# The last rows of a fused two-layer kernel: another order of quantising steps, and a deviation that moves from the rows into the scales

## What is computed

```python
x = x + _L1_attn_ref(_layernorm(x), ...)          # 16 heads of 128, causal, per half of 256 x 2 rows
# last layer, on n = layernorm(x):
x_max   = max(abs(n), axis=row)
x_scale = maximum(x_max / 127, 1e-12)
x_q     = clip(round(n / x_scale), -128, 127)     # int8
y       = (x_q @ w_q.T) * x_scale * w_scale + bias
x       = x + y
```

## Time and profile before

| | |
|---|---|
| median of 3 runs | 505.29 us (504.79 to 505.61) |
| the profiled execution's own time | 505.88 us |
| its span in the profile | 504.1 us, 8912 instructions |
| mean granted TensorE clock | 0.991 of full speed |
| busy PE, PEld | 482.8 us (96%), 429.8 us (85%) |
| busy DVE, ACT, POOL | 378.2 us (75%), 295.4 us (59%), 282.5 us (56%) |

### The profile page before, as it was taken

One profiled execution on the slowest core, in us unless ns is written; L12 is line 12 of the kernel. 1 busy time (PEld: TensorE's weight loads), 2 busy tenths in 40 slices (PEclk: granted clock), 3 DMA queues, 4 the chain that ended last, 5 costly groups with the idle time before them and its releaser, 6 DMA issues.

```text
span 504.1 us, 8912 instructions
## 1 busy us (share of the span) xinstructions
PE 482.8 (96%) x3020; PEld 429.8 (85%) x3020; DVE 378.2 (75%) x964; ACT 295.4 (59%) x694; POOL 282.5 (56%) x378
## 2 busy tenths in 40 slices
PE   8999999999999977899999999999999999999984
PEld 7888998899888856799888999899889989899972
DVE  2776776775746578788779888788878897667897
ACT  2355336535554645676667676667757766655663
POOL 1344244323665556786667786777767796511344
PEclk9999999999999999999999999999999999999996
DMA  9900000000010017564864764764765654100002
GB/s 278 380 22 2 1 0 1 0 1 1 24 42 1 0 46 184 159 187 109 213 182 127 195 181 114 210 179 122 202 178 149 177 170 131 36 1 1 0 2 83
DMA packets 54380, 51.58 MB, mean 102 GB/s; under 512 B 3520, under 2 KB 49728, under 8 KB 54336
## 3 DMA queue, kind: packets, MB, share of 16 engines
q1 hardware_dynamic: 53248, 49.98, 34.7%
q10 hardware_dynamic: 1088, 1.05, 0.6%
HBM read 32.92 MB, written 18.09 MB: 101 GB/s over the span
## 4 chain that ended last, share of the span: by engine, by line
PE 71%; DVE 13%; POOL 4%; issue 4%; DMA 3%; ACT 3%; SPq 1%; DVEq 0%; POOLq 0%; ACTq 0%
PE bank L405 19%; PE bank L407 18%; PE bank L406 18%; PE bank L700 3%; PE bank L698 3%; PE bank L699 3%; POOL HID_lo L1156 2%; DMA Wv_sb<-wv 2%; DVE BT L1535 2%; PE bank L628 1%; PE bank L627 1%; DVE SM L1516 1%; PE bank L709 1%; ACT E L906 1%; DMA turned_dram<-BT 1%
## 5 line engine op out<-in xcount | busy, mean ns | idle before, releaser
L1187 POOL TENSOR_TENSOR PT_lo<-MV,PT_hi 128x512 fp32r<-128x512 f32 (+1 forms) x104 | 91.5, 909 | 51.5 <-ACT PT_hi L998 51.1
L987 ACT ACTIVATE PR<-SM,nmax 128x128 f32<-128x128 f32 (+3 forms) x128 | 72.0, 563 | 62.6 <-DVE nmax L1516 62.1
L1132 POOL TENSOR_TENSOR E_lo<-E,E_hi 128x512 fp32r<-128x512 f32 x24 | 31.0, 1297 | 54.0 <-ACT E_hi L911 46.8
L1516 DVE CUSTOM_DVE_ANT_0 SM<-bank,causal 128x384 f32<-128x384 f32 (+3 forms) x102 | 54.0, 530 | 9.3 <-PE bank L700 6.4
L405 PE MATMUL bank<-XT_hi,W_hi 128*128 128x512 f32 x128 | 52.3, 409 | 5.2 <-DVE V_lo L1498 3.7
L998 ACT CAST PT_hi<-MV 128x512 fp32r<-128x512 f32 (+1 forms) x104 | 42.1, 453 | 19.6 <-DMA MV<-turned_dram 19.2
L1535 DVE STREAM_TRANSPOSE BT<-PR 128x128 f32<-128x128 f32 (+1 forms) x104 | 48.2, 492 | 5.6 <-POOL PR L1171 3.8
L407 PE MATMUL bank<-XT_hi,W_lo 128*128 128x512 f32 x128 | 50.5, 394 | 0.0
L406 PE MATMUL bank<-XT_lo,W_hi 128*128 128x512 f32 x128 | 50.2, 392 | 0.0
L406 PE MATMUL bank<-PT_lo,V_hi 128*128 128x128 f32 (+3 forms) x130 | 41.5, 319 | 0.0
L407 PE MATMUL bank<-PT_hi,V_lo 128*128 128x128 f32 (+3 forms) x130 | 41.5, 319 | 0.0
(11 more groups left out here) (189 smaller groups left out, 1602.6 us busy)
## 6 DMA issues: line engine op xcount, KB each, us to landing
MV<-turned_dram SPq DMA_DIRECT2D x104, 160.0 KB, 3.2
turned_dram<-BT SPq DMA_DIRECT2D x26, 384.0 KB, 2.9
stage<-pack SPq DMA_DIRECT2D x32, 256.0 KB, 3.9
turned_dram<-BT SPq DMA_DIRECT2D x26, 256.0 KB, 3.3
X<-x SPq DMA_DIRECT2D x2, 512.0 KB, 8.9
wraw<-wupT SPq DMA_DIRECT2D x1, 1024.0 KB, 9.6
wraw<-wgateT SPq DMA_DIRECT2D x1, 1024.0 KB, 11.5
wraw<-wdownT SPq DMA_DIRECT2D x1, 1024.0 KB, 13.7
```

The lines of the kernel that those rows point to most:

```text
L987: act.activation(PR[:, c, 0:(c + 1) * P], SM[:, c % 2, 0:(c + 1) * P], ACT.Exp, bias=nmax1[:, c:c + 1], scale=-1.0, accum_out=sum1[:, c:c ...
L1132: pool.tensor_tensor(E0_lo[:, m, :], E0[:, m, :], E0_hi[:, m, :], ALU.subtract).then_inc(e0_lo, 1)
L1187: pool.tensor_tensor(by_quad(PT_lo[w % 2], c), moved_part(w, c), by_quad(PT_hi[w % 2], c), ALU.subtract).then_inc(mv_lo, 1)
L1516: dve.tensor_tensor_reduce(SM[:, c % 2, 0:n], s_bank(w, c)[:, 0:n], mask, 1.0, HIGHEST, ALU.add, ALU.min, nmax1[:, c:c + 1]).then_inc(s_ma ...
```

## The change

Four things are changed.

1. On DVE, N2 and N3 move from the end of window 29 to behind S2 of that window, and X0, X1, X2 move from window 31 (behind T0 T1) to the end of window 29. `clip_first`, now called `clip_rounded(0)`, moves from behind the last window into window 31 as X3, behind T0 T1. On ACT, R0 moves to behind T0 T1 of window 31, and X0 ahead of A1. On PE, I0 moves ahead of P1 and F1, with a wait for `o_free`.
2. Half 1 is no longer normalised by DVE. DVE writes the negative means of two tiles (`row_means`), and ACT writes x - mean (`centre`, steps N0 and N1, either side of I1). `centred_absmax` takes the maximum, and `centred_scale` puts rs into both the scale and the inverse scale: four small instructions for each pair of tiles in place of two.
3. GpSimd rounds tiles 4 and 5: two `tensor_scalar` instructions, times the inverse scale plus the rounding constant. DVE then clips them with `clip_rounded(1)`. `clip_above` and `clip_below` are no longer called.
4. GpSimd adds the bias to tiles 4 to 7 of X only when ACT has read them.

```diff
-            WINDOWS - 1: steps("T0 T1 B0 T2 A0 T3 P0 F0 A1 P1 F1 I0 I1")}
+            WINDOWS - 1: steps("T0 T1 B0 T2 A0 T3 P0 F0 A1 I0 P1 F1 I1")}
...
-            WINDOWS - 1: steps("T0 T1 B0 T2 A0 T3 R0 A1 X0 I0 I1")}
+            WINDOWS - 1: steps("T0 T1 R0 B0 T2 A0 T3 X0 A1 I0 N0 I1 N1")}
...
-            WINDOWS - 3: steps("T0 T1 S0 W2 N0 Q0 T2 T3 S1 N1 S2 R0 K1 N2 S3 A0 R1 N3"),
+            WINDOWS - 3: steps("T0 T1 S0 W2 N0 Q0 T2 T3 S1 N1 S2 N2 N3 R0 K1 S3 A0 R1 X0 X1 X2"),
...
-            WINDOWS - 1: steps("T0 T1 X0 X1 X2 B0 T2 A0 T3 O0")}
+            WINDOWS - 1: steps("T0 T1 X3 B0 T2 A0 T3 O0")}
...
             def int8_turn(t0, t1):
 
+                if t0 == 0:
+                    pe.wait_ge(o_free, WINDOWS - 1)
...
+            def centre(g):
+
+                for t in range(*GROUPS[g]):
+                    act.wait_ge(ln_mean, g)
+                    act.activation(XN[:, t % CT, :], X[:, t, :], ACT.Identity, bias=ln_nm[:, t % CT:t % CT + 1],
+                                   scale=1.0).then_inc(centred, 1)
...
-                pool.wait_ge(ln_norm, CT * k + c1)
+                if k < 7:
+                    pool.wait_ge(ln_norm, CT * k + c1)
...
             rstd(7, 2, CT)
+            pool.wait_ge(q_inv, 2)
+            pool.wait_ge(q_round, 1)
+            for t in range(*GROUPS[1]):
+                last = pool.tensor_scalar(XQ1[:, t % CT, :], XN[:, t % CT, :], xinv[:, t:t + 1], ROUND, ALU.mult, ALU.add)
+            last.then_inc(q_clip, 1)
+            pool.wait_ge(centred, 2)
             add_bias(7, qb_bc, 0, 2)
             pool.wait_ge(q_round, 4)
+            pool.wait_ge(centred, CT)
             add_bias(7, qb_bc, 2, CT)
...
+            def row_means(g):
+                c0, c1 = (t - CT for t in GROUPS[g])
+                dve.tensor_scalar(ln_nm[:, c0:c1], ln_mv[:, c0:c1, 0], -1.0, None, ALU.mult).then_inc(ln_mean, 1)
+
+            def centred_absmax(g):
+                t0, t1 = GROUPS[g]
+                dve.wait_ge(centred, t1 - CT)
+                dve.tensor_reduce(xam[:, t0:t1], XN[:, t0 - CT:t1 - CT, :], AX.X, ALU.max,
+                                  apply_absolute_value=True).then_inc(q_absmax, 1)
+
+            def centred_scale(g):
+
+                t0, t1 = GROUPS[g]
+                rows, rs = slice(t0, t1), ln_rs[:, t0 - CT:t1 - CT]
+                done = 3 * g - 2
+                dve.wait_ge(q_absmax, g + 1)
+                dve.wait_ge(ln_rstd, 7 + g)
+                dve.scalar_tensor_tensor(xs[:, rows], xam[:, rows], 1.0 / QMAX, rs, ALU.mult, ALU.mult).then_inc(q_scale, 1)
+                dve.wait_ge(q_scale, done + 1)
+                dve.tensor_scalar(xs[:, rows], xs[:, rows], 1e-12, None, ALU.max).then_inc(q_scale, 1)
+                dve.wait_ge(q_scale, done + 2)
+                dve.reciprocal(xinv[:, rows], xs[:, rows]).then_inc(q_scale, 1)
+                dve.wait_ge(q_scale, done + 3)
+                dve.tensor_tensor(xinv[:, rows], xinv[:, rows], rs, ALU.mult).then_inc(q_inv, 1)
...
-            def clip_first():
-                dve.wait_ge(q_clip, 1)
-                dve.tensor_scalar(XQ2[:], XQ1[:], ROUND + QMAX, ROUND + QMIN, ALU.min, ALU.max).then_inc(q_round, 1)
+            def clip_rounded(g):
+                t0, t1 = GROUPS[g]
+                c = slice(t0 % CT, t0 % CT + t1 - t0)
+                dve.wait_ge(q_clip, g + 1)
+                if g == 1:
+                    dve.wait_ge(q_ready, CT)
+                dve.tensor_scalar(XQ2[:, c, :], XQ1[:, c, :], ROUND + QMAX, ROUND + QMIN, ALU.min,
+                                  ALU.max).then_inc(q_round, 1)
...
-            b0_quantise = (token_absmax, token_scale, token_inverse)
+            b0_quantise = (token_absmax, token_scale, token_inverse, clip_rounded)
...
             ln_variance(7, 0, 2)
+            row_means(1)
             z_low_half(1)
-            clip_first()
...
             ln_variance(7, 2, CT)
-            ln_normalise(7, 0, 2)
-            token_absmax(1)
-            token_scale(1)
-            token_inverse(1)
-            ln_normalise(7, 2, CT, 1)
-            clip_above(1)
-            token_absmax(2)
-            clip_below(1)
-            token_scale(2)
-            token_inverse(2)
+            row_means(2)
+            centred_absmax(1)
+            centred_scale(1)
+            centred_absmax(2)
+            centred_scale(2)
+            clip_rounded(1)
```

More of the change, by code:

```diff
@@ L96, in build @@
         ln_rs = sb("ln_rs", [P, CT])
+        ln_nm = sb("ln_nm", [P, CT])
         w_abs = sb("w_abs", [P, 3])
@@ L212, in build @@
         ln_rstd, ln_norm = sem("ln_rstd"), sem("ln_norm")
+        ln_mean, centred = sem("ln_mean"), sem("centred")
         xt_psum, xt_hi, xt_lo = sem("xt_psum"), sem("xt_hi"), sem("xt_lo")
@@ L1078, in window @@
                         round_first()
+                    elif kind == "N":
+                        centre(c + 1)
                     elif kind == "X":
```

## The result

The changed kernel took 508.31 us in the median of 7 runs (507.31 to 509.84), against 505.29 (504.79 to 507.00) for the kernel before in as many runs beside it: a ratio of 1.0058, 95% interval 1.0042 to 1.0073. It is slower; the forecast was 505.6 with a range up to 506.6. Its profiled execution took 507.31 us, with a span of 505.5.

A forecast was written before the change was run, and what follows sets the result against it. It took PE and DVE as full at the attention's end, with DVE's order setting the end. Terms 0.54 + 0.20 + 0.12 - 0.56 = +0.30 us, carried over to the median of 505.29, gave 505.6, range 504.3 to 506.6.

The forecast's parts named there:

- Term 1: End of window 29: X0 to X2 moved there on DVE delay window 30's first `PT_lo` and PE's values; +0.54 us.
- Rival A: Window 29: DVE's added work is covered because PE or ACT sets window 30's pace; 504.75 us, chance 0.20.
- D: Half 0: not finished two steps sooner, as its clip must wait for R0; counted as part of the forecast.
- Term 2: Window 31: half 0's round and clip ahead of `Z_lo`, clip lengthened beside GpSimd's additions; +0.20 us.
- Term 3: Ahead of half 1: I0 ahead of P1 costs nothing, the first `row_means` ahead of `Z_lo` costs +0.12 us.
- Term 4: Half 1 on DVE, from L1239 to the clip's end: 3.78 us instead of 4.34, so -0.56 us.
- Rival B: Half 1: eight dependent small DVE instructions in `centred_scale` take 0.40 us each instead of 0.21; 507.1 us, chance 0.12.
- Behind the clip: Half 1's outputs: about 0.1 us of slack given back, +0.1 for the clip beside GpSimd's additions; set off to nothing.
- GpSimd's rounding: Half 1: rounding two tiles takes 0.98 us, hidden within some 1.4 us before DVE asks for it.
- rival C: Half 1: GpSimd becomes the bound, its two tiles costing over 1.4 us; at 0.95 each 506.1 us, chance 0.06.

The follow-up runs named there:

- Late bias: The changed kernel, with GpSimd's bias additions to tiles 4 to 7 waiting for the second inverse scale; 508.81 us, 1.0055 against the kernel before.
- half 1 reordered: Kernel before's windows, half 1 by centring, with ACT's centrings and GpSimd's first two bias additions moved earlier, `ln_nm` declared last; 505.33 us, 1.0000 against the kernel before.
- PE kept busy: The changed kernel with `ln_nm` declared last, plus 16 idle PE products ahead of half 1's transposes; one run, tail 35.34 us.
- half 1 only: The kernel before with only the change's centring, scales and GpSimd rounding of half 1, orders of windows 29 to 31 as before; 509.35 us, ratio 1.0055.

## Why the prediction was wrong

It took the right places for the front, but mis-sized half 1 and the part behind the clip, and did not see that a declaration could cost. Against the sum's +0.30 us stand +1.66 in the tail and +0.80 in the feed-forward products between 130 and 191 us.

- **Term 1** (+0.54, bounds 0.45 to 0.75) held: the first `PT_lo` of window 30 came 0.77 later (forecast 0.75), PE's values 0.62. Rival A, that the front is free, is out. So is D: as forecast, the clip waited for R0 (0.82 us of idle DVE).
- **Term 2** (+0.20, bounds 0 to 0.4) was at +0.31 (`Z_lo` 0.93 later, less 0.62), inside its bounds, but by a clip of 1.06 us, outside of 0.68 to 0.95. The step "0.68 to 0.95" lengthened the clip in the proportion of the normalised tiles (1.02 us for two instead of 0.73). What the traces show is a wait for the end of GpSimd's instruction (495.12 beside 495.11, 496.50 beside 496.48), so the addend follows from what is left of that instruction and is no factor. The trace of before had it already: of the two tiles that took 1.02 us the first took 0.70, to 0.15 us behind the end of GpSimd's addition, and the second 0.40 behind that; the pair that was called alone had GpSimd's rs beside it (491.83, 0.79 us). With **Term 3** (+0.12) the front came to +1.06 against +0.86.
- **Term 4** (-0.56) is the step that failed. It took "four small instructions at 0.21" twice. The first chain was cheaper (0.68 us instead of 0.84), the second cost 1.71. The rest was as forecast: from `ln_ve` to the first maximum 0.15 instead of 0.29, the maxima 0.71, the clip 0.41. So 0.15 + 0.71 + 0.68 + 0.71 + 1.71 + 0.41 = 4.37 us. The prediction counted GpSimd's additions in for one clip of 1024 columns and did not ask who runs beside the small instructions, though it put GpSimd's rounding and additions there in the next paragraph. "The cost at two columns is that of the instruction itself" holds beside an idle GpSimd only (0.16 or 0.17 us). Rival B had this size (0.40 in the mean, here 1.71 / 4 = 0.43) in one chain of the two, with another cause: not the dependence, which cost nothing in the first chain. Late bias and half 1 reordered show the cause.
- **Behind the clip** (set to 0) cost 0.57. The forecast named the low granted clock only as a danger to ACT's centring. It saw that half 0's PE work moves forward, but not that half 1's transposes would then come after 4.38 us of idle PE, at half the clock. The run with PE kept busy shows the price. That the old order escapes it is partly luck of the profile: its five profiles average 5.67, so that 0.38 of the 0.57 is left against them.
- **GpSimd's rounding** (hidden, 0.98 us) took 0.93 and no one waited for it; rival C is out. It was costly as a neighbour, not as work. Of ACT's centring "little is left over" was right: with the old front (half 1 only) DVE waited 1.38 us for it.
- **A line the prediction costed at nothing without saying so** is the declaration of `ln_nm`: 16 bytes among the first tiles, +0.80 us between 130 and 191 us, where the change edits no instruction. "Each part of the change" must take in the declarations.

The two measured losses, 1.66 and 0.80, make 2.46 of the 3.02 us between the medians; the interval of the ratio, 2.1 to 3.7 us, holds it. In the profiled pair alone the second does not show in the end: the changed kernel lost the 0.80 and still reached the mark 0.18 us earlier, by the spread of the attention windows between.

## What to carry to other kernels

When work is moved to GpSimd, ask what VectorE does at that time. Here its `TENSOR_TENSOR`, `SCALAR_TENSOR_TENSOR` and `TENSOR_SCALAR` of 128x2 on tiles in SBUF waited for the end of GpSimd's rounding or addition (0.44, 0.41 and 0.67 us instead of 0.16 or 0.17), so a chain of tiny ones can pay for each. What cost nothing here was to have GpSimd's long instructions beside VectorE's reductions (0.68 us for 128x512 beside the rounding) and reciprocals (0.17 beside an addition), beside its reads of PSUM (`PT_lo` of 128x384 took 0.55 us beside the additions in the trace of before and 0.56 without them), or in its idle time. Where an early PE step is moved still earlier, look at the gap that it leaves and at the clock of what comes behind the gap (4.38 us and 0.50 here). Declare a new small tile behind all others (61.07 us for the stretch from 130 to 191 us instead of 61.89), and when a kernel slows where nothing was edited, compare the mean of its PE groups before looking for a wait.

## What the runs showed of the hardware that was not expected

- With sixteen bytes of unused memory ahead of the operands the products of `T_down` with `HID_lo` (256 columns) took 281 ns instead of 279, and those of `XT_hi` with `T_gate` (512 columns) 395 instead of 391, at the full clock; the stretch of 61 us was 0.8 us longer. With 64 bytes they took 281 and 391 ns, with 512 bytes 279 and 391.
- A VectorE instruction on 128x2 took up to 0.67 us instead of 0.17 beside GpSimd's rounding and additions, while `RECIPROCAL` and `TENSOR_REDUCE` beside them kept their 0.17 and 0.68.
- In two profiles of the kernel before, the granted clock near the end was low (0.50) from 24.9 to 28.3 us behind the mark and again from 31.7 in one, and only from 31.3 in the other.
